# A transformer block on one core: the inverse row sums are scaled as two rows of three read and three rows of two written

## The chip, the cores and the metric

The kernel runs on 1 core of one Trainium2 chip. The metric is the device time of an execution in microseconds (us). One execution was also recorded by the profiler; instruction durations come from that one. In what follows PE is TensorE (PEld is its weight load), DVE is VectorE, ACT is ScalarE, POOL is GpSimd and SP is SyncE, which issues all the DMAs.

## The reference, cut to what matters

For x of 16 batches x 512 tokens x 256 channels:

```
xn = layernorm(x)
q, k, v = xn @ wq, xn @ wk, xn @ wv        # 8 heads of 128
q, k = rope(q), rope(k)
s = q k^T / 128, causal mask               # 512 x 512 per batch and head
p = softmax(s)
attn = (p v) @ wo
ffn = s2 * relu2(s1 * relu2(s0 * [xn, -xn] @ K0) @ K1) @ K2     # K are +1/-1, relu2 is 2 * relu
out = x + attn + ffn
```

The softmax is what the change touches: each row of p is exp(s - max) divided by the sum of the row.

## The kernel before, in words

The core works through 128 groups g = 8b + h, one for each batch b and head h. Precision beyond 16 bits comes from splitting a value into a high and a low fp16 part: ACT writes the high part, DVE the rest, and PE multiplies high by high, high by low and low by high.

Of a group, PE computes q and k (`qk`, whose matmuls are recorded at L277), ACT, DVE and POOL rotate them (L485, L486, L637, L417, L641, L489, L420), and PE forms the scores (`scores`, L763) in four tiles of 128 queries, whose widths are 128, 256, 384 and 512 because of the causal mask. The four tiles i = 0 to 3 of a group lie in three PSUM banks. Then, for the softmax:

- `row_max` (DVE, L665) masks a tile and keeps the row maximum in column i of the four of `MX`, in slot g % 4.
- `row_bias` (ACT, L502) turns the four maxima into the four biases in `NM`.
- `exponent` (ACT, L506) takes the exponential of a tile in place and accumulates the row sums into column i of `SM`.
- `inverse` (DVE, L672 to L676) is a reciprocal of the four sums (L673) and, after a wait for it, a multiplication by 4096 (L675). `RI`, the reciprocals, is the same memory as `NM`, and `RK`, the scaled ones, is that of `MX`. The scaling reads and writes its four values in the order 0, 2, 1, 3, as two rows of two with a stride of two inside a row.
- `p_hi` (ACT, L510) writes the high part of the normalised tile, with the scaled value of the row as its scale; it waits for `inverse` by the semaphore s_inv. `p_lo` (DVE, L679) writes the low part, after the `p_hi` of the same tile.
- SP turns the tiles round by DMA transposes (L325), and PE multiplies by v (`values`, L780). ACT and DVE split the result (`o_hi` L499, `o_lo` L660), and PE projects it with wo (`project`).

Beside this PE works on the feed-forward net: `layer0` (L277), the seven half-size products that stand for the eight of layer 1 (`product`, L812) and `layer2` (L823). The product with wv is also made of seven (`v_product`, L801), and DVE copies or adds its partial sums from bank to bank in between (`copy_v`, L647; `add_v5`, L644). POOL normalises the next batch (L385) and makes its sums (L398 to L403).

Nothing is scheduled at run time. Each engine has one program, written out by hand as a sequence of helper calls with semaphore waits between them; batches 4 to 14 are one loop body. Each engine issues strictly in that order, so what stands behind a slow instruction on its engine waits with it. Two places of the vector program matter below. In the loop body (L4672 and after) the order is

```
copy_v(dve, ps[0], ps[7])
dve.wait_ge(s_exp, 32 * b + 4)
inverse(dve, 8 * b)
dve.wait_ge(s_P_hi, 32 * b + 1)
p_lo(dve, 8 * b, 3, ps[3])
dve.wait_ge(s_vs, 14 * b - 5)
dve.wait_ge(s_ffn, 2 * b)
copy_v(dve, ps[0], ps[6])
```

and a `v_product` of PE waits for that second `copy_v`. In batch 1 to 2, `inverse` of group 12 is followed by a `row_max` and an `o_lo`, and `scores` on PE wait for that `o_lo` to free a bank.

Of the kernel before, what the change touches and what calls it, by code (L numbers as in the profile page):

```python
# [10 lines left out]
ALU = mybir.AluOpType  # L11
ACT = mybir.ActivationFunctionType
# [7 lines left out]
HI, LO = 0, 1  # L20
# [17 lines left out]
def block_kernel(nc, x, wq, wk, wv, wo, k0, k1, k2, s3, cosT, sinT, out):  # L38
    ctx = ExitStack()
    with ctx:  # L40
        def sb(name, shape, dt=F32):
            return ctx.enter_context(nc.sbuf_tensor(name, shape, dt))

        def sem(name):
            return ctx.enter_context(nc.semaphore(name))
# [27 lines left out]
        LESS = HALF[:, 4:5]  # L73
        MX = sb("mx", [128, 4, 4])
        NM = sb("nm", [128, 4, 4])
        SM = sb("sm", [128, 4, 4])
        RI = NM
        RK = MX
        P2 = sb("p2", [128, 4])
        KN = sb("kn", [128, 4])  # L80
        SC = sb("sc", [128, 8])
# [93 lines left out]
        s_exp = sem("s_exp")  # L175
        s_inv = sem("s_inv")
        s_P_hi = sem("s_P_hi")
# [42 lines left out]
        s_recip = sem("s_recip")  # L220
# [22 lines left out]
        def tile_of(ps, i):  # L243
            return ps[:, S_COL[i]:S_COL[i] + WIDTH[i]]

        def part(g, i, s):
            q, row, n = SQUARE[i]
            a = SQ_AT[q] + s * SQ_SIZE[q] + row * n * 128
            return PH[:, g % 2, a:a + WIDTH[i]]
# [251 lines left out]
        def row_bias(act, g):  # L501
            act.activation(NM[:, g % 4, :], MX[:, g % 4, :], ACT.Copy, scale=SC[:, 1:2]).then_inc(s_bias, 1)  # L502

        def exponent(act, g, i, ps):
            p = tile_of(ps, i)
            act.activation(p, p, ACT.Exp, bias=NM[:, g % 4, i:i + 1], scale=SC[:, 0:1],  # L506
                           accum_out=SM[:, g % 4, i:i + 1]).then_inc(s_exp, 1)

        def p_hi(act, g, i, ps):
            act.activation(part(g, i, HI), tile_of(ps, i), ACT.Copy, scale=RK[:, g % 4, i:i + 1]).then_inc(s_P_hi, 1)  # L510

        def keep_r(act, ps):
            act.activation(RT[:, 0:2].rearrange("p a b -> p (a b)"), ps[:, :], ACT.Relu).then_inc(s_r, 1)
# [27 lines left out]
        def stats_end(dve, b):  # L541
            r = b % 2
            for t in range(4):
                mv = dve.bn_aggr(MV[:, r, t, :], BN[:, t, :])
            mv.then_inc(s_mean, 1)
            dve.wait_ge(s_mean, b + 1)
            dve.tensor_scalar(VE[:, r, :], MV[:, r, :, 1], EPS, 2.0 ** -12, ALU.add, ALU.mult).then_inc(s_stats, 1)

        def stats_first(dve):
            for t in range(2):  # L550
                stats_tile(dve, 0, t)
            dve.wait_ge(s_x[0], 16)
            stats_tile(dve, 0, 2)
            stats_tile(dve, 0, 3).then_inc(s_rows, 1)
            dve.wait_ge(s_rows, 1)
            stats_end(dve, 0)

        def stats(dve, b):
            for t in range(4):
                rows = stats_tile(dve, b, t)  # L560
            rows.then_inc(s_rows, 1)
            dve.wait_ge(s_rows, b + 1)
            stats_end(dve, b)
# [102 lines left out]
                                     scalar=-3.0e38, op0=ALU.add, op1=ALU.max,  # L666
                                     accum_out=MX[:, g % 4, i:i + 1]).then_inc(s_max, 1)

        def every_other(v):
            return v.rearrange("p (a b) -> p b a", a=2)  # L670

        def inverse(dve, g):  # L672
            dve.reciprocal(RI[:, g % 4, :], SM[:, g % 4, :]).then_inc(s_recip, 1)  # L673
            dve.wait_ge(s_recip, g + 1)
            dve.tensor_scalar(every_other(RK[:, g % 4, :]), every_other(RI[:, g % 4, :]), 4096.0, None,  # L675
                              ALU.mult).then_inc(s_inv, 1)  # L676

        def p_lo(dve, g, i, ps):
            dve.scalar_tensor_tensor(part(g, i, LO), tile_of(ps, i), RK[:, g % 4, i:i + 1], part(g, i, HI),  # L679
                                     ALU.mult, ALU.subtract).then_inc(s_P_lo, 1)  # L680

        def difference(dve, n, ps):
# [914 lines left out]
        def scalar_program(act):  # L1597
# [107 lines left out]
            v_first_hi(act, 0, 2, BANK[3])  # L1705
            act.wait_ge(s_bias, 1)
            exponent(act, 0, 3, BANK[4])
            exponent(act, 0, 2, BANK[2])
            exponent(act, 0, 0, BANK[2])
            exponent(act, 0, 1, BANK[5])  # L1710
            act.wait_ge(s_v, 2)
            v_first_hi(act, 0, 0, BANK[6])
            act.wait_ge(s_inv, 1)
            p_hi(act, 0, 3, BANK[4])
            p_hi(act, 0, 2, BANK[2])
            act.wait_ge(s_rot, 6)
            qk_hi(act, 2, 1)
            p_hi(act, 0, 0, BANK[2])
            p_hi(act, 0, 1, BANK[5])
            act.wait_ge(s_max, 8)  # L1720
# [1549 lines left out]
            o_hi(act, 127, BANK[5])  # L3270

        def vector_program(dve):
            dve.wait_ge(s_x_first, 16)
            dve.wait_ge(s_x[0], 16)
            stats_first(dve)
# [122 lines left out]
            row_max(dve, 1, 2, BANK[7])  # L3398
            dve.wait_ge(s_exp, 4)
            inverse(dve, 0)  # L3400
            dve.wait_ge(s_crossed, 6)
            dve.wait_ge(s_straight, 6)
            rotate(dve, 2, 1, BANK[1])
            row_max(dve, 1, 0, BANK[7])
            dve.wait_ge(s_P_hi, 1)
            p_lo(dve, 0, 3, BANK[4])
            dve.wait_ge(s_S, 6)
            row_max(dve, 1, 1, BANK[1])
            v_first_lo(dve, 0, 0, BANK[6])
            dve.wait_ge(s_P_hi, 4)  # L3410
            p_lo(dve, 0, 1, BANK[5])
            p_lo(dve, 0, 0, BANK[2])
            p_lo(dve, 0, 2, BANK[2])
            v_first_lo(dve, 0, 2, BANK[3])
            split_w_lo(dve, "v", 4)
            dve.wait_ge(s_exp, 8)
            inverse(dve, 1)
            v_first_lo(dve, 0, 3, BANK[6])
            dve.wait_ge(s_swap, 7)
# [26 lines left out]
            v_first_lo(dve, 1, 2, BANK[4])  # L3446
            dve.wait_ge(s_exp, 12)
            inverse(dve, 2)
            split_w_lo(dve, "v", 5)
            dve.wait_ge(s_o_hi, 1)  # L3450
# [1022 lines left out]
            for b in range(4, 15):  # L4473
                ps = [BANK[i] for i in ROTATION[b]]
# [1999 lines left out]
        @block.vector  # L6474
        def _(e):
            vector_program(e)
# [33 lines left out]
```

## Time and profile before

| | us |
|---|---|
| runs shown (3) | 1725.69, 1727.59, 1727.61 |
| median | 1727.59 |
| the profiled execution's own time | 1725.82 |
| span of its instructions | 1724.0 |
| PE busy in the span | 1701.0 (99%) |
| DVE busy | 1465.5 (85%) |
| ACT busy | 1482.5 (86%) |
| POOL busy | 970.5 (56%) |
| granted TensorE clock, mean | 0.997 of full speed |

A busy PE is not PE at its peak, since matmuls overlap in the pipeline. So a short wait of PE is not to be seen as idle time of PE, but as a larger distance between the starts of two groups of matmuls. The profiled execution lies 1.77 us under the median of the runs shown.

### The profile page before, as it was taken

To read this page: it belongs to the slowest core of one execution; us is meant where nothing else is said; L and a number is where in the kernel's file an instruction comes from. 1 tells how busy PE (TensorE), PEld (TensorE's weight loads), DVE (VectorE), ACT (ScalarE), POOL (GpSimd) and SP (SyncE) were. 2 spreads that over 40 slices of the span, in tenths; PEclk is the share of its full clock that TensorE was granted. 3 is DMA by queue.
4 is the path that set the end of the run, shared out by engine and by line. 5 is a ranking of instruction groups with operands and counts; after the bars stand their busy time and mean duration, and the time that the engine had idled before them with its cause. 6 is when DMAs were issued, how large, how long until landed. Compare 5 with 4: busy or idle time off the path is not lost.

```text
span 1724.0 us, 35729 instructions
## 1 busy us (share of the span) xinstructions
PE 1701.0 (99%) x13340; PEld 1257.8 (73%) x13340; DVE 1465.5 (85%) x3502; ACT 1482.5 (86%) x3250; POOL 970.5 (56%) x775
## 2 busy tenths in 40 slices
PE   7999999999999999999999999999999999999999
PEld 3567767777777687777777777777777777768777
DVE  8998798888988889788897888879888898887975
ACT  6898898888988889888898888888888898888984
POOL 7764647556564565655556465564655656455522
PEclk9999999999999999999999999999999999999999
DMA  5233644534434344453435434344453434434443
GB/s 177 47 71 63 113 77 84 95 62 96 77 83 77 81 80 75 93 75 74 87 73 99 74 80 88 72 82 81 88 83 68 92 74 93 68 80 80 75 83 72
DMA packets 486044, 142.03 MB, mean 82 GB/s; under 512 B 465904, under 2 KB 484848, under 8 KB 485872
## 3 DMA queue, kind: packets, MB, share of 16 engines
q1 hardware_dynamic: 485872, 139.76, 42.5%
q8 instruction: 105, 1.72, 0.4%
q14 instruction: 67, 0.55, 0.1%
HBM read 14.94 MB, written 8.39 MB: 14 GB/s over the span
## 4 chain that ended last, share of the span: by engine, by line
PE 94%; DVE 4%; ACT 1%; DMA 0%; issue 0%; SPq 0%; POOL 0%; DVEq 0%
PE bank L277 35%; PE bank L812 21%; PE bank L780 12%; PE bank L763 11%; PE bank L801 8%; PE bank L823 6%; DVE bank L665 1%; DVE ph L679 0%; ACT bank L506 0%; ACT ph L510 0%; DMA pt<-ph 0%; DVE bank L637 0%; DVE tb L641 0%; PE bank L791 0%; DVE hb L629 0%
## 5 line engine op out<-in xcount | busy, mean ns | idle before, releaser
L417 POOL TENSOR_TENSOR tb<-tb,sin 128x512 f32<-128x512 f32 x256 | 325.7, 1275 | 274.6 <-ACT tb L486 272.8
L420 POOL TENSOR_TENSOR qk<-tb,qk 128x512 f16<-128x512 f32 x256 | 296.7, 1165 | 326.0 <-ACT qk L489 325.8
L812 PE MATMUL bank<-hb,wa 128*128 128x256 f16 x3360 | 382.2, 273 | 0.0
L812 PEld LDWEIGHTS bank<-hb,wa 128*128 128x128 fp8e5 x3360 | 327.5, 98 | 38.9
L506 ACT ACTIVATE bank<-bank,nm,sc 128x512 f32<-128x512 f32 (+3 forms) x512 | 301.3, 589 | 2.9
L679 DVE SCALAR_TENSOR_TENSOR ph<-bank,mx,ph 128x256 f16<-128x256 f32 (+3 forms) x512 | 251.4, 542 | 27.8 <-ACT ph L510 27.1
L510 ACT ACTIVATE ph<-bank,mx 128x512 f16<-128x512 f32 (+3 forms) x512 | 231.0, 537 | 25.8 <-DVE mx L675 25.7
L665 DVE CUSTOM_DVE_ANT_0 bank<-bank,mask 128x128 f32<-128x128 f32 (+3 forms) x512 | 237.1, 513 | 15.4 <-PE bank L763 15.2
L763 PE MATMUL bank<-qk 128*128 128x512 f16 (+3 forms) x1536 | 230.4, 299 | 4.9 <-DVE tb L641 2.6
L780 PE MATMUL bank<-pt,v 128*128 128x256 f16 (+1 forms) x2304 | 229.2, 255 | 1.5 <-DVE hb L692 0.6
L780 PEld LDWEIGHTS bank<-pt,v 128*128 128x128 f16 x2304 | 202.1, 98 | 29.0 <-issue 3.5
L485 ACT ACTIVATE tb<-bank 64x512 f32<-64x512 f32 x256 | 152.2, 594 | 79.8 <-PE bank L277 72.1
L637 DVE TENSOR_TENSOR bank<-bank,cos 128x512 f32<-128x512 f32 x256 | 178.3, 701 | 29.4 <-ACT tb L486 29.0
L763 PEld LDWEIGHTS bank<-qk 128*128 128x128 f16 x1536 | 132.9, 98 | 95.5 <-DVE tb L641 2.8
L489 ACT ACTIVATE qk<-tb 128x512 f16<-128x512 f32 x256 | 160.4, 634 | 33.8 <-PE bank L763 28.5
L277 PE MATMUL bank<-xT,wk 128*128 128x512 f16 x768 | 187.3, 381 | 0.1
L277 PE MATMUL bank<-xT,wq 128*128 128x512 f16 x768 | 186.0, 379 | 0.4 <-DVE ph L679 0.4
L641 DVE TENSOR_TENSOR tb<-bank,tb 128x512 f32<-128x512 f32 x256 | 173.4, 683 | 14.3 <-POOL tb L417 9.9
L277 PE MATMUL bank<-wo,o 128*128 128x256 f16 x1536 | 172.9, 273 | 0.0
L277 PEld LDWEIGHTS bank<-wo,o 128*128 128x128 f16 x1536 | 150.3, 98 | 18.0
L424 POOL TENSOR_TENSOR hb<-rt,hb 128x1024 f16<-128x1024 f32 x60 | 127.9, 2132 | 60.6 <-ACT hb L522 60.6
L486 ACT ACTIVATE tb<-bank 64x512 f32<-64x512 f32 x256 | 150.9, 589 | 3.0
(140 smaller groups left out, 2627.7 us busy)
## 6 DMA issues: line engine op xcount, KB each, us to landing
out<-xnat SPq DMA_DIRECT2D x32, 256.0 KB, 2.1
xnat<-in_x SPq DMA_DIRECT2D x15, 512.0 KB, 3.8
pt<-ph SPq DMA_TRANSPOSE x256, 4.3
o<-in_k SPq DMA_DIRECT2D x1, 1024.0 KB, 7.6
v<-in_wq SPq DMA_DIRECT2D x1, 1024.0 KB, 9.6
v<-in_wk SPq DMA_DIRECT2D x1, 1024.0 KB, 11.5
ph<-in_wv SPq DMA_DIRECT2D x1, 1024.0 KB, 14.0
o<-in_wo SPq DMA_DIRECT2D x1, 1024.0 KB, 10.9
```

The costliest lines, as they stand in the source:

```text
L277: m = pe.matmul(ps[:, cols[0]:cols[1]], l, r, start=start and n == 0, stop=signal is not None and n == last)
L417: pool.tensor_tensor(tb, tb, SIN[:], ALU.mult).then_inc(s_crossed, 1)
L420: pool.tensor_tensor(QK[:, g % 2, 2 * w + 1, :], TB[:, (2 * g + w) % TRING, :], QK[:, g % 2, 2 * w, :], ALU.subtract).then_inc(s_qk_lo, 1)
L506: act.activation(p, p, ACT.Exp, bias=NM[:, g % 4, i:i + 1], scale=SC[:, 0:1], accum_out=SM[:, g % 4, i:i + 1]).then_inc(s_exp, 1)
L510: act.activation(part(g, i, HI), tile_of(ps, i), ACT.Copy, scale=RK[:, g % 4, i:i + 1]).then_inc(s_P_hi, 1)
L637: dve.tensor_tensor(ps[:, :], ps[:, :], COS[:], ALU.mult).then_inc(s_straight, 1)
L641: dve.tensor_tensor(tb, ps[:, :], tb, ALU.add).then_inc(s_rot, 1)
L665: dve.tensor_tensor_reduce(out=s, in0=s, in1=MASK[:, 512 - WIDTH[i]:512], scale=1.0, scalar=-3.0e38, op0=ALU.add, op1=ALU.max, accum_out=M ...
L679: dve.scalar_tensor_tensor(part(g, i, LO), tile_of(ps, i), RK[:, g % 4, i:i + 1], part(g, i, HI), ALU.mult, ALU.subtract).then_inc(s_P_lo, 1)
L763: mm = pe.matmul(ps[:, col:col + w], l, m, start=i == tiles[0] and n == 0, stop=end)
L780: mm = pe.matmul(ps[:, 128 * i0:128 * i1], l, m, start=n == 1, stop=n == 18)
L812: mm = pe.matmul(ps[:, 256 * u:256 * u + 256], WA[:, w, k, (2 * j + u) * 128:(2 * j + u) * 128 + 128], HB[:, h, s, k, :], start=first and ...
```

## The change

`SM`, `RI` and `RK` become buffers of their own. The sums and the reciprocals lie in two rows of four places, of which three are used: tile i is at row i // 3, column i % 3. The reciprocal reads and writes all six used places. The scaling reads them as two rows of three and writes them as three rows of two, so the scaled value of tile i is at row i // 2, column i % 2. Two of the six values belong to no tile; one memset at the start of the vector program makes the whole of `SM` ones. No wait is added, moved or taken away.

```
-        SM = sb("sm", [128, 4, 4])
-        RI = NM
-        RK = MX
+        SM = sb("sm", [128, 4, 2, 4])
+        RI = sb("ri", [128, 4, 2, 4])
+        RK = sb("rk", [128, 4, 3, 4])
...
+        def row_sum(g, i):
+            return SM[:, g % 4, i // 3, i % 3:i % 3 + 1]
+
+        def row_scale(g, i):
+            return RK[:, g % 4, i // 2, i % 2:i % 2 + 1]
...
             act.activation(p, p, ACT.Exp, bias=NM[:, g % 4, i:i + 1], scale=SC[:, 0:1],
-                           accum_out=SM[:, g % 4, i:i + 1]).then_inc(s_exp, 1)
+                           accum_out=row_sum(g, i)).then_inc(s_exp, 1)
...
-            act.activation(part(g, i, HI), tile_of(ps, i), ACT.Copy, scale=RK[:, g % 4, i:i + 1]).then_inc(s_P_hi, 1)
+            act.activation(part(g, i, HI), tile_of(ps, i), ACT.Copy, scale=row_scale(g, i)).then_inc(s_P_hi, 1)
...
+        def unused_sums(dve):
+            dve.memset(SM[:], 1.0)
...
-        def every_other(v):
-            return v.rearrange("p (a b) -> p b a", a=2)
-
         def inverse(dve, g):
-            dve.reciprocal(RI[:, g % 4, :], SM[:, g % 4, :]).then_inc(s_recip, 1)
+            dve.reciprocal(RI[:, g % 4, :, 0:3], SM[:, g % 4, :, 0:3]).then_inc(s_recip, 1)
             dve.wait_ge(s_recip, g + 1)
-            dve.tensor_scalar(every_other(RK[:, g % 4, :]), every_other(RI[:, g % 4, :]), 4096.0, None,
-                              ALU.mult).then_inc(s_inv, 1)
+            dve.tensor_scalar(RK[:, g % 4, :, 0:2], RI[:, g % 4, :, 0:3], 4096.0, None, ALU.mult).then_inc(s_inv, 1)
...
-            dve.scalar_tensor_tensor(part(g, i, LO), tile_of(ps, i), RK[:, g % 4, i:i + 1], part(g, i, HI),
+            dve.scalar_tensor_tensor(part(g, i, LO), tile_of(ps, i), row_scale(g, i), part(g, i, HI),
                                      ALU.mult, ALU.subtract).then_inc(s_P_lo, 1)
...
         def vector_program(dve):
+            unused_sums(dve)
             dve.wait_ge(s_x_first, 16)
```

## Rows read from the trace of the kernel before

**Rows 1.** The page: busy time by engine.
```profile
PE 1701.0 (99%) x13340; PEld 1257.8 (73%) x13340; DVE 1465.5 (85%) x3502; ACT 1482.5 (86%) x3250; POOL 970.5 (56%) x775
```

**Rows 2.** Groups on DVE: busy us, mean ns of one | idle before.
```profile
L675 DVE TENSOR_SCALAR mx<-nm 128x4 f32<-128x4 f32 x128 | 41.4, 323 | 4.4
...
L614 DVE RECIPROCAL kn<-p 128x2 f32<-128x2 f32 x2 | 0.3, 166 | 0.1
...
L568 DVE TENSOR_SCALAR pt<-pt 128x3 f32<-128x3 f32 x1 | 0.2, 199 | 0.0
```

**Rows 3.** Single lines: duration ns min/median/max.
```profile
L675 DVE TENSOR_SCALAR mx<-nm x128: 169/170/1140, 65.5 to 1704.6; 128x4 f32<-128x4 f32 x128
...
L673 DVE RECIPROCAL nm<-sm x128: 160/177/179, 65.3 to 1704.4; 128x4 f32<-128x4 f32 x128
...
L547 DVE TENSOR_SCALAR ve<-mv x16: 170/538/1266, 6.3 to 1554.8; 128x4 f32<-128x4 f32 x16
```

**Rows 4.** Stretches, L675 alone: us, DVE busy (count), clock, DMA share, GB/s.
```profile
864.50:969.50 105.00, 2.85 (x8) 1.00 0.43 79
```

**Rows 5.** Stretches, PE alone: us, PE busy (count), clock, DMA share, GB/s.
```profile
864.50:969.50 105.00, 105.00 (x837) 1.00 0.43 79
```

**Rows 6.** Order of time around 884 us, batch 8: start, duration, engine, line.
```profile
884.15 1.15 POOL L420 TENSOR_TENSOR qk<-tb,qk 128x512 f16<-128x512 f32 x1 [2.11 <-ACT qk L489]
...
884.46 0.87 DVE L675 TENSOR_SCALAR mx<-nm 128x4 f32<-128x4 f32 x1
...
886.09 0.75 DVE L679 SCALAR_TENSOR_TENSOR ph<-bank,mx,ph 128x512 f16<-128x512 f32 x1 [0.76 <-ACT ph L510]
...
886.69 0.82 PE L801 MATMUL bank<-wv,xT 128*128 128x256 f16 x6
886.75 0.69 DVE L647 TENSOR_SCALAR bank<-bank 128x512 f32<-128x512 f32 x1
...
887.50 0.83 PE L801 MATMUL bank<-wv,xs 128*128 128x256 f16 x6
```

**Rows 7.** The chain of waits, batches 0 to 2: start us, us, what.
```profile
84.35 0.61 DVE mx L675
...
95.37 0.93 DVE mx L675
...
119.44 0.65 PE bank L801 x6
...
215.99 1.14 DVE mx L675
```

**Rows 8.** Waits of the weight loads: us in total, times, longest.
```profile
PEld bank L801 <- DVE bank L647: 4.9, 14, 1.3
```

**Rows 9.** Order of time around 84 us.
```profile
84.87 1.29 DVE L617 SCALAR_TENSOR_TENSOR wv<-o,kn,wv 128x512 f16<-128x512 f32 x1
84.89 0.73 POOL L398 TENSOR_TENSOR xs<-xs 128x256 f32<-128x256 f32 x1
...
86.91 1.79 PE L763 MATMUL bank<-qk 128*128 128x512 f16 x12 [0.65 <-DVE o L660]
```

**Rows 10.** Order of time around 96 us and 110 us.
```profile
95.14 0.62 ACT L489 ACTIVATE qk<-tb 128x512 f16<-128x512 f32 x1
...
96.33 1.42 ACT L510 ACTIVATE ph<-bank,mx 128x128 f16<-128x128 f32 x3 [0.56 <-DVE mx L675]
...
110.44 0.81 PE L780 MATMUL bank<-pt,v 128*128 128x256 f16 x6 [0.64 <-DVE hb L692]
```

**Rows 11.** Order of time around 216 us.
```profile
217.18 1.31 ACT L510 ACTIVATE ph<-bank,mx 128x512 f16<-128x512 f32 x3
...
218.39 1.16 PE L763 MATMUL bank<-qk 128*128 128x384 f16 x9 [1.56 <-DVE o L660]
...
218.91 0.47 DVE L679 SCALAR_TENSOR_TENSOR ph<-bank,mx,ph 128x256 f16<-128x256 f32 x1
```

**Rows 12.** The last inverse, order of time.
```profile
1704.61 0.17 DVE L675 TENSOR_SCALAR mx<-nm 128x4 f32<-128x4 f32 x1
```

## The prediction

> **What bounds the kernel now.** I read the page first. PE is busy 99% of the span, DVE and ACT 85% [rows 1], so only a wait that reaches PE costs time. The groups on DVE then show what the change is about: the scaling L675 has 128 instructions of 323 ns on average [rows 2], though the single line gives a median of 170 ns and a maximum of 1140 ns [rows 3]. Most take 170 ns; a few take far longer. The sum over the clean time is 41.4 - 128 x 0.170 = 19.6 us. The reciprocal L673 just ahead of it, as small and also from buffer to buffer, never takes more than 179 ns [rows 3]. The small L547 behaves as the scaling does: 170 at least, 1266 at most [rows 3]. In order of time each long scaling overlaps a POOL instruction: that of 884.46 runs 0.87 us and ends at 885.33, just as the POOL L420 of 884.15 ends (885.30) [rows 6]. So the scaling waits for POOL to finish, the reciprocal doesn't.
>
> The Trainium skill says the same of the engines (VectorE: DVE Perf Modes, "Mode 2×_2P — use both read ports for one tensor"; SBUF — State Buffer, "Who interferes with whom"): a tensor_scalar between SBUF buffers uses a port pair shared with GpSimd, and waits for it, if the outermost dimensions of source and destination are both even, or equal. By that rule the old pattern (two and two) waits, as the rows show, and the new one (two and three) wouldn't.
>
> In the steady part eight scalings take 2.85 us a batch [rows 4], 1.49 over 8 x 0.170: two long ones. Over the same 105.00 us PE is busy 105.00 [rows 5]. There almost all of the DVE time saved is hidden. What is left is read from distances between PE groups, and from the chain for the first three batches, which holds three long scalings [rows 7].
>
> **The steady part.** Around 884.46 the order on DVE is scaling, p_lo (waiting for p_hi on ACT), copy_v. p_lo starts at 886.09 and copy_v right behind it at 886.75, and PE's next v_product starts at 887.50, when copy_v has ended [rows 6]. The v_product before it started at 886.69, a distance of 0.81, where six such matmuls take 0.65 when nothing is waited for [rows 7]: PE lost 0.16 us. With a scaling of about 0.2 us, p_hi, p_lo and copy_v move up by 0.67. p_lo would end near 886.17 and copy_v near 886.8, ahead of the 887.34 at which PE could go on. So this whole 0.16 goes, and the next limit is PE itself. The waits of the weight loads for L647 are 14, 4.9 us in sum, one of 1.3 [rows 8]: the other 13 are alike, 0.28 each (seen at the load, which runs ahead of the matmul), one a batch. 13 x 0.16 = **2.1 us**. The other long scaling of a batch has no distance behind it on PE over the free one: 0.
>
> **The first batches.** Up to 110 us the chain runs mostly on DVE.
> - 84.35: 0.61 us [rows 7], of which 0.44 is waiting. Next on DVE is L617, itself held up: 1.29 us beside POOL's L398 [rows 9]. Started earlier, it would meet the POOL instruction that the scaling met and go behind it, POOL's L398 then waiting instead. It ends some 0.4 to 0.5 earlier, and so do the o_lo behind it and PE's scores at 86.91, which wait for that o_lo [rows 9]. I take 0.45. POOL may lose up to 0.7 us once; its results are next needed by ACT and a transpose, with more than that to spare.
> - 95.37: 0.93 us, 0.76 of it waiting. ACT is busy with L489 to 95.76, so p_hi, now at 96.33, gains 0.57 at most [rows 10]. I take 0.5.
> - PE waits for DVE at 110.44 with 0.64 of visible idle time [rows 10], so both gains arrive there: 0.95. Behind it the stretch to 136 us hangs on PE's own products, which come earlier by as much.
> - 215.99: 1.14 us, 0.97 of it waiting [rows 7]. Behind it on DVE stand a row_max and the o_lo that PE waits for until 218.39, 1.56 of visible idle time [rows 11]. That o_lo moves up by nearly 0.9. But the next steps of PE wait for p_lo of group 12. ACT's p_hi at 217.18 does not move, since ACT has had work all the time before it. PE's `values` wait for the p_lo of 218.91, which ends at 219.38 [rows 11]; without the delayed o_lo in front it would end at about 219.0. Of 0.9, PE keeps **0.4**.
> The other long one there, at 204 us, lies beside a PE that has work.
> Sum of the head: **1.35 us**, between 0.7 (the chain cuts the first two to half, the third to 0.2) and 2.2 (all of 0.44, 0.76 and 0.97).
>
> **What it adds.** The reciprocal has six values for four. Two values take 166 ns and four 173 on average [rows 2, 3], so about 7 ns more. The scaling of six isn't in the trace: at least as now (170), at most the slowest clean small one, 199 ns for three values [rows 2]; I take 185. That is 128 x 22 ns = 2.8 us on DVE, hidden but at some 5 places of the head and the last inverse, whose scaling is clean now (0.17) [rows 12]: 6 x 0.02 = 0.1 us. A gain from a scaling under 170 ns is excluded, as no 4-value one is faster. The memset is one instruction while DVE waits for x: 0. Were x there at once, it would cost what a small instruction does, 0.2. The buffers of their own add no wait and take none away: 0.
>
> **Sum.** 2.1 + 1.35 - 0.1 = 3.35 us of the profiled execution's 1725.82: 1722.5. That execution lies 1.8 us under the median of the runs shown, whose two upper values are 1727.6. I forecast against the median: 1727.59 - 3.35 = **1724.2 us**. A measurement of this kernel can tell about 0.2%, 3.45 us, from no change; the forecast lies on that edge.
>
> **The rivals.**
> - **A, the forecast** (0.60). Scalings free of POOL, 2.6 to 4.1 us gained. Half of it is on either side of 3.45, a little more below it: 0.27 faster, 0.33 same.
> - **B, the head gives all**: 2.1 + 2.2 - 0.1 = 4.2 us, 1723.4. For it: the chain puts all three long scalings on the critical path [rows 7]. Against it: ACT's gapless work at 95.7 and 217.2 [rows 10, 11]. 0.12, faster.
> - **C, given back later**: PE arrives earlier at a wait that now just passes (a transpose, POOL's rotation), and only the steady 2.1 or the head's 1.35 is left: 1725.5 to 1726.2. For it: hundreds of PE waits are met now with a margin that the rows don't show. 0.16, same.
> - **D, the change does not do what it says**: the new pattern waits for POOL as well. The trace has no instruction with unlike patterns; only that L673 escapes shows that size and place are not what makes one wait. Then 1727.59 + 0.1 = 1727.7. 0.09, same.
> - **E, slower**: six values read as rows of three and written as rows of two run as a slow form. The place is the scaling in front of copy_v, once a batch. It lasts 0.87 there now; PE loses nothing while it is under 0.71, loses the present 0.16 at 0.87, and every nanosecond above counts. To be 3.45 slower over 13 batches takes 1.14 us a scaling; the time would be 1731. The nearest small instructions without POOL take 0.2 [rows 2]. 0.03.
>
> **How the numbers follow.** Faster by over 0.2%: 0.27 + 0.12 = 0.39. Same: 0.33 + 0.16 + 0.09 = 0.58. Slower: 0.03. The range: the largest gain, 4.2, taken from the lower runs (1725.7) gives 1721.5; the smallest gain of C, 1.35, from the upper (1727.6) gives 1726.3, and I reach on to 1727.3 for a part of D.
>
> **What would show it.** In the changed kernel the scaling should have a minimum and a maximum close to each other, 170 to 200 ns, and 24 us or less in sum for 41.4; ACT's 0.5 us waits for it shrink. The reciprocal stays under 190. L547 keeps its long ones, being untouched. In a steady batch the two v_products around 886.7 stand 0.65 apart, the weight loads no longer wait for L647, and a batch's period falls by 0.16. In the head PE's group at 110.44 comes at about 109.5. Wrong would be: long scalings that remain (D); a period unchanged though the scalings are short (the wait passed to another instruction, C); a PE wait for copy_v that stays, because copy_v waits for its own product and not for p_lo.

## The result, and the profile after

| | before | changed |
|---|---|---|
| median of 21 runs each, us | 1728.08 | 1725.25 |
| lowest and highest, us | 1725.69, 1730.61 | 1721.22, 1727.03 |
| profiled execution, us (span) | 1725.82 (1724.0) | 1725.58 (1723.8) |
| granted TensorE clock of it | 0.997 | 0.995 |

The ratio of the runs is 0.998, with a 95% interval of 0.9974 to 0.9986: 3.5 us less, between 2.4 and 4.5. The medians differ by 2.83 us. The interval leaves out 1, so the gain is there; but the ratio lies just on the 0.2% that the forecast had as its edge.

The two profiled executions differ by 0.24 us only, so they must be compared stage by stage. First the scaling itself. The page's busy times, then single lines of the changed kernel (duration ns min/median/max; L681 is the scaling, L679 the reciprocal; the line between them is what ACT's p_hi waited for the scaling, us in total and times), and the scaling in one steady stretch (us, DVE busy, clock, DMA share, GB/s):

```profile
PE 1701.2 (99%) x13340; PEld 1259.8 (73%) x13340; DVE 1450.5 (84%) x3503; ACT 1481.1 (86%) x3250; POOL 969.9 (56%) x775
```

```profile
L681 DVE TENSOR_SCALAR rk<-ri x128: 159/160/161, 68.7 to 1704.2; 128x6 f32<-128x6 f32 x128
...
  ACT ph L516: 10.9, 18
...
L679 DVE RECIPROCAL ri<-sm x128: 173/190/192, 68.5 to 1704.0; 128x6 f32<-128x6 f32 x128
```

```profile
864.50:969.50 105.00, 1.27 (x8) 1.00 0.42 79
```

The maximum of the scaling fell from 1140 ns [rows 3] to 161, its mean from 323 [rows 2] to 160, and the eight of a batch take 1.27 us for 2.85 [rows 4]. The 128 scalings take 20.9 us less in sum and the reciprocals 1.6 more; DVE's busy time on the page, where instructions that overlap count once, falls by 15.0. PE is as busy as before [rows 1]. The new memset runs at 0.80 us for 0.09, long before x arrives at 4.34, and costs nothing.

In the kernel before, 29 scalings start with over 0.3 us of a POOL instruction still to run. 27 of them are the long ones, and each of these ends 22 to 25 ns after that POOL instruction; the two others (at 65.5 and 193.9 us, beside POOL's L385) stay short, and why isn't shown. In the changed kernel 29 scalings start so as well, and none takes over 161 ns. (In both kernels 54 reciprocals start beside a POOL instruction, and all are short.) Around the place in front of copy_v (L656 now), in order of time, with POOL's L420 running from 884.93 to 886.08, as long as before:

```profile
884.93 1.15 POOL L420 TENSOR_TENSOR qk<-tb,qk 128x512 f16<-128x512 f32 x1 [2.12 <-ACT qk L489]
885.03 0.18 DVE L679 RECIPROCAL ri<-sm 128x6 f32<-128x6 f32 x1
885.24 0.16 DVE L681 TENSOR_SCALAR rk<-ri 128x6 f32<-128x6 f32 x1
...
886.83 0.69 DVE L656 TENSOR_SCALAR bank<-bank 128x512 f32<-128x512 f32 x1
...
887.46 0.82 PE L806 MATMUL bank<-wv,xT 128*128 128x256 f16 x6
...
888.12 0.82 PE L806 MATMUL bank<-wv,xs 128*128 128x256 f16 x6
```

The scaling is done in 0.16 us while POOL still runs. copy_v ends at 887.52, PE needs it at 888.12, and the two v_products stand 0.66 apart, not 0.81 [rows 6]. The waits of the weight loads for copy_v were 14 with 4.9 us [rows 8]; two are left, the long one and one of 0.3 (us in total, times, longest):

```profile
PEld bank L806 <- DVE bank L656: 1.6, 2, 1.3
```

Then PE as a whole. Both kernels have the same 13340 matmuls in the same order, so the start of the n-th one can be compared. The table has, for each kernel, by how many us PE is later than in the kernel before (a minus: earlier), at ten matmuls that start in the kernel before at the times in the first line. e1 to e10 are the experiments of the next section. (Only differences between columns of a line say something of the change. What comes in the first 81 us differs from execution to execution, as shown below.)

```
at            42    81    87    98   110   218   361  1519  1705  1720
changed     3.17  3.12  2.44  2.05  1.77  1.61  1.61 -0.41 -0.40 -0.28
e1          1.70  3.05  3.06  3.06  3.06  3.06  3.06  3.03  3.04  3.13
e2          1.99  3.35  3.34  3.34  3.34  3.33  3.33  3.25  3.25  3.12
e3          1.98  2.49  2.48  2.48  2.48  2.46  2.46  2.36  2.36  2.21
e4          2.24  2.05  1.36  0.98  0.69  0.51  0.52 -1.46 -1.47 -1.54
e5          2.65  2.61  2.61  2.61  2.61  2.61  2.61  0.59  0.59  0.43
e6          2.39  3.73  3.05  2.66  2.40  2.23  2.23  2.27  2.27  2.14
e7          1.63  0.60 -0.09 -0.47 -0.74 -0.90 -0.90 -2.37 -2.37 -2.47
e8          2.58  2.50  1.81  1.42  1.14  0.97  0.97  3.99  3.98  3.85
e9          1.85 -0.24 -0.93 -1.31 -1.59 -1.76 -1.76 -3.79 -3.80 -3.84
e10         0.88  0.84  0.15 -0.24 -0.52 -0.69 -0.69 -2.47 -2.48 -2.25
```

In the changed kernel PE is 3.12 us late at 81 us and gains from there on: 1.51 by 218 us (0.68, 0.39, 0.28 and 0.16 at the four matmuls of 87, 98, 110 and 218 us), nothing to 361, then 2.02 in twelve steps of 0.167, one a batch and each at the v_product behind copy_v. From 81 us to the end it gains 3.40 us.

**Where the 3.1 us of the first 81 us come from.** Stretches of PE, the kernel before and then the changed one (us, PE busy, granted clock, DMA share, GB/s):

```profile
0.00:45.00 45.00, 33.89 (x152) 0.92 0.50 170
```

```profile
0.00:45.00 45.00, 33.13 (x138) 0.85 0.50 170
```

The granted clock of the first 45 us was 0.92 of full speed in the one and 0.85 in the other: more of that time at 1.2 GHz, for 2.4. In this part PE waits again and again for loads and for DVE, and each trace has stretches at half clock after such waits, in other places and of other length each time. The clock is not all of it. By 14 us PE is 0.9 us late already, at full clock in both: ACT's L439 starts at 11.27 us after 1.04 us of waiting for the load of `in_k`, for 10.37 in the kernel before, where it waited for no load, and the first xT that PE needs comes 0.9 later with it. In the other ten executions of the table the same instruction starts between 10.20 and 11.12. None of this touches an inverse, the first of which comes at 65 us. So the first column of the table, from 0.88 to 3.17, says nothing of the change: the changed kernel itself stands at both ends of it (3.17, and e10 with 0.88).

The 21 runs spread alike: those of the changed kernel with a mean clock of 0.993 took 1726.5 us (mean of 3), with 0.995 1724.0 (4), with 0.997 1722.1 (2). Only the profiled executions show where the low clock lies: within the first 81 us nearly all of it.

### The profile page after: what moved, and what is told of

Its sections match the earlier page's. It is cut to its first block, busy times and chain, and to the rows that moved or that the text cites. A ratio compares the mean times of both kernels' runs of the same rounds, so it can differ in the third digit from the quotient of the medians.

```text
span 1723.8 us, 35730 instructions
## 1 busy us (share of the span) xinstructions
PE 1701.2 (99%) x13340; PEld 1259.8 (73%) x13340; DVE 1450.5 (84%) x3503; ACT 1481.1 (86%) x3250; POOL 969.9 (56%) x775
## 4 chain that ended last, share of the span: by engine, by line
PE 95%; DVE 2%; ACT 1%; DMA 1%; issue 0%; SPq 0%; DVEq 0%
PE bank L277 36%; PE bank L817 21%; PE bank L785 12%; PE bank L768 12%; PE bank L806 8%; PE bank L828 6%; DMA o<-in_k 0%; PE bank L796 0%; DVE bank L674 0%; ACT bank L512 0%; ACT ph L516 0%; DMA pt<-ph 0%; DVE ph L684 0%; DVE hb L638 0%; DVE rt L689 0%
## 5 line engine op out<-in xcount | busy, mean ns | idle before, releaser
L420 POOL TENSOR_TENSOR qk<-tb,qk 128x512 f16<-128x512 f32 x256 | 296.9, 1166 | 326.2 <-ACT qk L489 326.0
L684 DVE SCALAR_TENSOR_TENSOR ph<-bank,rk,ph 128x256 f16<-128x256 f32 (+3 forms) x512 | 251.5, 543 | 27.8 <-ACT ph L516 27.1
L516 ACT ACTIVATE ph<-bank,rk 128x512 f16<-128x512 f32 (+3 forms) x512 | 231.0, 538 | 11.1 <-DVE rk L681 10.9
L489 ACT ACTIVATE qk<-tb 128x512 f16<-128x512 f32 x256 | 160.2, 633 | 33.8 <-PE bank L768 28.5
```

Of the source, the lines that this page charges most:

```text
L420: pool.tensor_tensor(QK[:, g % 2, 2 * w + 1, :], TB[:, (2 * g + w) % TRING, :], QK[:, g % 2, 2 * w, :], ALU.subtract).then_inc(s_qk_lo, 1)
L684: dve.scalar_tensor_tensor(part(g, i, LO), tile_of(ps, i), row_scale(g, i), part(g, i, HI), ALU.mult, ALU.subtract).then_inc(s_P_lo, 1)
```

## The experiments

All start from the changed kernel unless said otherwise. Most were timed by one execution, whose time says little when those of one kernel differ by up to 5 us; for these the trace and the table carry the reading.

**e1: buffers of their own, nothing else** (edited from the kernel before)

```
         SM = sb("sm", [128, 4, 4])
-        RI = NM
-        RK = MX
+        RI = sb("ri", [128, 4, 4])
+        RK = sb("rk", [128, 4, 4])
```

> The kernel before, with buffers of their own for the reciprocals and the scaled values, and nothing else; the scaling keeps its two rows of two. My theory (the pattern does it): the scaling keeps its long ones, 16 to 18 of over 0.5 us, about 41 us in sum as before, the v_product behind copy_v stays 0.81 us behind the one before it, and the time is that of before. Rival (sharing memory with NM and MX made the scaling wait): all 128 at 0.16 to 0.17 us, 21 us in sum.

One execution of 1728.93 us, the kernel before beside it at 1728.07 (median). Single line, as above:

```profile
L675 DVE TENSOR_SCALAR rk<-ri x128: 169/170/1136, 67.2 to 1707.6; 128x4 f32<-128x4 f32 x128
```

28 scalings over 0.3 us (27 in the kernel before; the 16 to 18 over 0.5 of my expectation were a miscount, it is 27 in both), 42.1 us in sum, and the line e1 of the table stays at 3.03 to 3.13 from 81 us to the end. Sharing memory had nothing to do with it, and the buffers alone move nothing.

**e2: patterns alike, two rows of three; e3: alike, three rows of two**

```
-        RK = sb("rk", [128, 4, 3, 4])
+        RK = sb("rk", [128, 4, 2, 4])
...
-            return RK[:, g % 4, i // 2, i % 2:i % 2 + 1]
+            return RK[:, g % 4, i // 3, i % 3:i % 3 + 1]
...
-            dve.tensor_scalar(RK[:, g % 4, :, 0:2], RI[:, g % 4, :, 0:3], 4096.0, None, ALU.mult).then_inc(s_inv, 1)
+            dve.tensor_scalar(RK[:, g % 4, :, 0:3], RI[:, g % 4, :, 0:3], 4096.0, None, ALU.mult).then_inc(s_inv, 1)
```

e3 keeps `RK` and makes `SM` and `RI` three rows as well, of which two places each are used:

```
-            dve.reciprocal(RI[:, g % 4, :, 0:3], SM[:, g % 4, :, 0:3]).then_inc(s_recip, 1)
+            dve.reciprocal(RI[:, g % 4, :, 0:2], SM[:, g % 4, :, 0:2]).then_inc(s_recip, 1)
...
-            dve.tensor_scalar(RK[:, g % 4, :, 0:2], RI[:, g % 4, :, 0:3], 4096.0, None, ALU.mult).then_inc(s_inv, 1)
+            dve.tensor_scalar(RK[:, g % 4, :, 0:2], RI[:, g % 4, :, 0:2], 4096.0, None, ALU.mult).then_inc(s_inv, 1)
```

> The changed kernel, but the scaling writes two rows of three, as it reads them: six values, own buffers, ones in the unused sums, and the patterns alike with an even outermost count. My theory (only unlike outermost counts keep the scaling clear of POOL): long scalings come back, 0.9 us at most of those in a steady batch, 1.5 us over the clean time a batch; the clean ones take 0.17, not 0.16; the time is that of the kernel before, 3 us over the changed one. Rival (six values, or rows that don't touch, are enough): all at 0.16, time of the changed kernel.

> The changed kernel with three rows of two on both sides of the scaling: the outermost counts are odd and equal. By the Trainium skill's rule (both even, or equal) it waits for POOL again: long ones of 0.9 us in a steady batch, 41 us in sum or little over. Rival (an odd outermost count on either side is enough to stay clear): all at 0.16, 20.4 us in sum.

e2 took 1727.99 us (median of 10), a ratio to the kernel before of 0.9999 (0.999 to 1.0009). e3, one execution, took 1728.02. Their scalings:

```profile
L681 DVE TENSOR_SCALAR rk<-ri x128: 170/171/1124, 67.5 to 1707.9; 128x6 f32<-128x6 f32 x128
...
  ACT ph L516: 35.0, 44
```

```profile
L681 DVE TENSOR_SCALAR rk<-ri x128: 169/170/1124, 67.5 to 1707.0; 128x6 f32<-128x6 f32 x128
```

Six values, own buffers and gaps between the rows are all there, and the whole gain is gone: the table's lines e2 and e3 are flat. Even and alike waits, odd and alike waits too. Both have 40 long scalings, 50.7 and 50.5 us in sum, more than the 41 I had expected of e3; all 80 end 24 to 31 ns after a POOL instruction. A third one a batch waits (766 ns at 941.36 in e2), which in the kernel before is clean (169 ns at 938.05). There POOL is between two instructions just as the scaling arrives, and the scaling arrives 0.02 us later behind the start of its reciprocal (0.23 for 0.21), which takes longer with six values; POOL's next one starts 0.24 behind it in both. That those 0.02 us decide which goes first is a guess and was not tried.

**e4: the patterns turned round**, three rows of two read (`SM` and `RI` have three rows, as in e3) and two rows of three written (`RK` has two, as in e2):

```
-            dve.tensor_scalar(RK[:, g % 4, :, 0:2], RI[:, g % 4, :, 0:3], 4096.0, None, ALU.mult).then_inc(s_inv, 1)
+            dve.tensor_scalar(RK[:, g % 4, :, 0:3], RI[:, g % 4, :, 0:2], 4096.0, None, ALU.mult).then_inc(s_inv, 1)
```

> The changed kernel with the patterns turned round: the scaling reads three rows of two and writes two rows of three. My theory (only the inequality of the outermost counts matters): all 128 at 0.16 us, 20.4 us in sum, time and chain as of the changed kernel. Rival (an even count on the reading side is what keeps clear, or the writing side alone decides): long ones as before, 40 of over 0.3 us.

```profile
L681 DVE TENSOR_SCALAR rk<-ri x128: 158/159/161, 67.8 to 1703.2; 128x6 f32<-128x6 f32 x128
```

1724.28 us in one execution, and from 81 us to the end PE gains 3.59 us, as in the changed kernel. So it is the inequality that counts, not the side. Together with e2 and e3 this agrees with the Trainium skill's condition (VectorE: DVE Perf Modes, "Mode 2×_2P — use both read ports for one tensor"). Counts that are both even but unequal were not tried. And with six values the rows differ in length whenever they differ in number, so these runs can't tell a rule on the number of rows from one on any unlike shape.

**e5: the new pattern in one scaling a batch (that of group 8b, from batch 3 on); e6: in all the others**

```
+        def free(g):
+            return g % 8 == 0 and g >= 24
...
+            to = RK[:, g % 4, :, 0:2] if free(g) else RL[:, g % 4, :, 0:3]
+            dve.tensor_scalar(to, RI[:, g % 4, :, 0:3], 4096.0, None, ALU.mult).then_inc(s_inv, 1)
```

`row_scale` reads `RK` or `RL` by the same condition; e6 has `not (...)`.

> The changed kernel, in which only the scaling of group 8b in front of copy_v, from batch 3 on, has the new pattern; all others read and write two rows of three. My theory: that one scaling a batch carries the whole steady gain. The distance of the two v_products falls from 0.81 to 0.65, 0.16 a batch, 12 times 0.167 = 2.0 us; the other long one of a batch (0.95 us) stays and costs nothing; the gains of the first 110 us are missing (1.4 us), so the time lies between the two kernels, 1.4 us over the changed one. Rival (both long scalings of a batch matter): less than 0.16 gained a batch.

> The complement of the run with one a batch: the scaling in front of copy_v from batch 3 on reads and writes two rows of three, all the others have the new pattern. My theory: the gains of the first 220 us are there (1.6 us), the steady gain is missing, so 12 distances of 0.81 between the v_products remain and this run ends 2.0 us later than the changed kernel on equal clocks. Rival (the other long one of a batch also carried a part): less than 0.16 lost a batch.

One execution each, 1726.23 and 1727.94 us. The table tells more: e5 stands at 2.61 up to 361 us and is at 0.59 at 1519, a gain of 2.02, all in the steady part, from 13 scalings with the new pattern and 115 with that of e2. e6 gains 1.50 from 81 to 218 us (3.73 to 2.23) and then stands still to 1705. 2.02 and 1.50 make 3.52, for the 3.40 and 3.59 of the two full ones. In e6 the scaling in front of copy_v and the v_products of batch 8 are as before:

```profile
886.72 0.86 DVE L688 TENSOR_SCALAR rl<-ri 128x6 f32<-128x6 f32 x1
...
888.94 0.82 PE L813 MATMUL bank<-wv,xT 128*128 128x256 f16 x6
...
889.75 0.83 PE L813 MATMUL bank<-wv,xs 128*128 128x256 f16 x6
```

0.81 again, and so (0.81 or 0.82) in all 12 batches from 3 to 14, for 0.65 or 0.66 in the changed kernel and e5. Of the 128 scalings, 12 carry the steady gain, one a batch.

**e7 and e8: a delay in front of that scaling**, 13 times in all: in batches 3 to 14 and, beyond the 12 that I had counted, in the last:

```
+            if g % 8 == 0 and g >= 24:
+                dve.memset(IDLE[:, 0:400], 1.0)
             dve.tensor_scalar(RK[:, g % 4, :, 0:2], RI[:, g % 4, :, 0:3], 4096.0, None, ALU.mult).then_inc(s_inv, 1)
```

`IDLE` is 480 fp16 values wide; e8 fills all of it, once before the reciprocal and once here.

> The changed kernel with one memset of 400 fp16 values on DVE between reciprocal and scaling of group 8b, from batch 3 on (12 in all): some 0.45 us of delay. PE would reach the v_product behind copy_v 0.54 us after copy_v is ready (888.12 less 0.06 less 887.52). My theory: the slack takes it all, the v_products stay 0.65 apart, nothing is lost. Rival (the whole DVE delay comes through, since DVE is 84% busy): 12 times 0.45 = 5.4 us more.

> The same with two memsets of 480 fp16 values, one ahead of the reciprocal and one ahead of the scaling: some 1.0 to 1.1 us of delay. My theory: 0.54 of it is taken by the slack, so PE loses 0.5 to 0.55 us a batch, 12 times that = 6 to 7 us; each waiting nanosecond over the slack counts. Rival (none comes through, PE has other work): the time of the changed kernel. Other rival (all comes through): 12 to 13 us.

The memsets took 392 ns, and twice 458; in batch 8 the scaling ends 0.37 us late in e7 and 0.95 in e8, measured from the start of the reciprocal or, for e8, of the copy_v ahead of both memsets. e7 keeps its v_products 0.65 or 0.66 apart in all 12 batches:

```profile
884.95 0.82 PE L809 MATMUL bank<-wv,xT 128*128 128x256 f16 x6
...
885.61 0.60 PE L809 MATMUL bank<-wv,xs 128*128 128x256 f16 x4
```

Its steady gain is 1.47 us for 2.02, but none of the 0.55 is lost at this place: 0.38 is one single wait of `values` for a transpose at 1062 us, which no other execution here has (e10 loses 0.18 to one like it at 538 us). e8:

```profile
888.92 0.82 PE L811 MATMUL bank<-wv,xT 128*128 128x256 f16 x6
...
889.99 0.83 PE L811 MATMUL bank<-wv,xs 128*128 128x256 f16 x6 [0.25 <-DVE bank L657]
```

1.07 apart, 0.42 lost; by the table e8 loses 3.02 us between 361 and 1519 us where the changed kernel gains 2.02, a difference of 5.04, which is 12 times 0.42. A delay of 0.95 less a loss of 0.42 is a slack of 0.53, for 0.54 by the rows of the changed kernel. I had expected 0.5 to 0.55 lost, the memsets having been estimated too long. So a delay of 0.37, under the slack, costs nothing, and of one of 0.95 all that is over the slack is lost.

**e9: the same for the variances.** The other small scaling that waits for POOL (L547 of [rows 3]) gets the same pattern; POOL's power behind it still takes four values. The two unused places of `MV` are made ones, and what reads `MV` and `VE` finds its values at the new places.

```
-        MV = sb("mv", [128, 2, 4, 2])
-        VE = sb("ve", [128, 2, 4])
+        MV = sb("mv", [128, 2, 2, 4, 2])
+        VE = sb("ve", [128, 2, 3, 4])
...
-            dve.tensor_scalar(VE[:, r, :], MV[:, r, :, 1], EPS, 2.0 ** -12, ALU.add, ALU.mult).then_inc(s_stats, 1)
+            dve.tensor_scalar(VE[:, r, :, 0:2], MV[:, r, :, 0:3, 1], EPS, 2.0 ** -12, ALU.add, ALU.mult).then_inc(s_stats, 1)
```

> The changed kernel, and the same pattern for the other small DVE instruction that waits for POOL, the variance scaling of the next batch (L553 there: 0.17 at least, 1.27 at most): it reads two rows of three and writes three rows of two. My theory: all 16 take 0.16, so the one of 1.27 us at 65.6 us ends 1.1 us earlier; it stands on the chain in front of the rotation that PE waits for (2.64 us of visible idle time). PE is 0.9 to 1.1 us earlier from there on, nothing more is gained in the steady part, where the variance is not waited for: some 1.0 us under the changed kernel, 4.4 under the one before. Rival (given back in the first 110 us at the next wait, on ACT's exponentials or POOL's rotation): less than 0.3 us.

> The changed kernel itself, timed on the same chip beside the one before and the run with the variance scaling. 3.4 us (0.2%) under the kernel before by the median, with each kernel's own runs spread over some 4 us as the TensorE clock of the first 75 us falls out; at equal granted clock the difference is 3 to 4 us.

| | median, us | ratio to before, interval |
|---|---|---|
| before (16 runs) | 1728.36 | |
| changed (11 runs) | 1725.10 | 0.998, 0.9971 to 0.9988 |
| e9 (6 runs) | 1722.76 | 0.9968, 0.9956 to 0.998 |

e9 is 2.3 us under the changed kernel by the medians; the intervals overlap a little. Its trace, order of time, behind the single line:

```profile
L554 DVE TENSOR_SCALAR ve<-mv x16: 160/161/161, 6.2 to 1551.0; 128x6 f32<-128x6 f32 x16
```

```profile
64.26 0.16 DVE L554 TENSOR_SCALAR ve<-mv 128x6 f32<-128x6 f32 x1
66.41 0.69 DVE L653 TENSOR_TENSOR tb<-bank,tb 128x512 f32<-128x512 f32 x1
67.15 0.22 PEld L771 LDWEIGHTS bank<-qk 128*128 128x128 f16 x3 [1.77 <-DVE tb L653]
67.16 0.50 PE L771 MATMUL bank<-qk 128*128 128x256 f16 x3 [1.60 <-DVE tb L653]
```

PE's idle time in front of those scores is 1.60 us. In the changed kernel it is 2.64:

```profile
69.52 0.82 PE L768 MATMUL bank<-qk 128*128 128x256 f16 x3 [2.64 <-DVE tb L650]
```

So 1.04 us were gained there, as expected. The rest is the clock. PE's stretches from 60 to 81 us, the changed kernel timed again (e10) and e9:

```profile
60.00:81.00 21.00, 17.93 (x109) 0.92 0.24 46
```

```profile
60.00:81.00 21.00, 18.62 (x123) 1.00 0.30 57
```

After the wait of 2.64 us PE ran for a while at half its clock (1.2 GHz): the matmuls of k behind it start 427 ns apart, where they take 216 otherwise. After the one of 1.60 us it did not, and that is worth 1.0 us more; e9 goes from 1.85 in the table at 42 us to -0.24 at 81. It isn't shown that the shorter wait is the reason: in e7 the wait was as long as ever (2.65), and the clock stayed at 1.00 too. From 81 us on e9 gains 3.60 us, no less than the changed kernel, so the rival (given back in the first 110 us) falls. Of the 2.3 us by the medians, then, 1.04 are shown to be the pattern's.

## Why the prediction was right

By its own steps:

- **What the scaling waits for, and that the new pattern ends it** (0.88 given to A, B and C together): right. e1 to e4 take the change apart: not the buffers, not the six values, not the gaps, only the unlike patterns do it.
- **The steady part, 2.1 us**: 2.02, by 12 places of 0.167 and not 13 of 0.16. The thirteenth wait of 0.28 stayed, so it wasn't the scaling's. The reading of it, that 0.16 of 0.70 us reaches PE and a slack hides the rest, is shown by e5, e6, e7 and e8: the point from which the scaling costs PE, 0.71 us long by rival E, is 0.16 + 0.53 = 0.69.
- **The head, 1.35 us**: 1.51, but not as summed. At 87 us 0.68 for 0.45, at 98 and 110 us together 0.67 for 0.5. L617 (L626 now) behaved as drawn: beside the POOL instruction that the scaling had waited for it takes 1.03 us, and POOL's L398 takes 1.18 for 0.73 [rows 9]:

```profile
87.49 0.16 DVE L681 TENSOR_SCALAR rk<-ri 128x6 f32<-128x6 f32 x1
87.57 1.03 DVE L626 SCALAR_TENSOR_TENSOR wv<-o,kn,wv 128x512 f16<-128x512 f32 x1
...
88.01 1.18 POOL L398 TENSOR_TENSOR xs<-xs 128x256 f32<-128x256 f32 x1
```

The scaling gives back the 0.44 of the prediction, and L617, which lasted 1.29, another 0.26 that the prediction had not counted. At the second place ACT set the bound, as said, but the bound of 0.57 was misread: p_hi starts 0.10 before the end of L489, in the changed kernel 0.52 after a start of L489 that lasts 0.62. So p_hi moved up by 0.67, and all of it reached PE.
- **The third place of the head, 0.4 us, is the step that failed**: 0.16. I had the row_max behind the scaling start at once. In the changed kernel DVE stands idle for 0.70 us in front of it. The kernel before, then the changed one:

```profile
216.02 0.81 PE L763 MATMUL bank<-qk 128*128 128x512 f16 x3
...
217.04 0.69 DVE L665 CUSTOM_DVE_ANT_0 bank<-bank,mask 128x512 f32<-128x512 f32 x1
```

```profile
217.79 0.81 PE L768 MATMUL bank<-qk 128*128 128x512 f16 x3
...
218.64 0.70 DVE L674 CUSTOM_DVE_ANT_0 bank<-bank,mask 128x512 f32<-128x512 f32 x1 [0.70 <-PE bank L768]
...
220.00 1.16 PE L768 MATMUL bank<-qk 128*128 128x384 f16 x9 [1.40 <-DVE o L669]
```

It needs scores that PE has only just made: it starts 0.04 us after they end (218.60), where it started 0.21 after them (216.83) in the kernel before. The difference, 0.17, is what PE gains. The long scaling had covered a wait for PE; the question "what is late next" was put to ACT and not to the instruction right behind.

- **What it adds**: a scaling of six takes 160 ns. I had excluded anything under 170. The alike six of e2 take 170 or more, so the ten nanoseconds belong to the pattern, not to the count. The reciprocal takes 186 for 173, twice what I took. No loss of PE is seen from either, so the term of 0.1 us was one too many.
- **Rival B** (all of the head, 2.2 us) and **C** (given back): 1.51 arrived, and no later wait took it back. **D** is ruled out by the 161 ns, **E** by the same.
- **The sum**: 3.35 us forecast, 3.40 in the trace from 81 us on, 3.09 in the repeated one (e10), 3.5 by the ratio and 2.83 by the medians. That it came within 0.05 of the trace is in part luck: two places of the head were put 0.40 us too low together and 0.1 was taken off that nothing cost; against that the third place was put 0.24 too high and the steady part 0.08, and 0.12 was lost in the last 20 us, which scatter by more than that from execution to execution (the last two columns of the table). The time, 1724.2 for 1725.25, is 1.05 off: 0.49 since the median of the kernel before is 1728.08 over 21 runs and not the 1727.59 of three, and 0.52 since the medians differ by less than 3.35. The ratio lies on the 0.2% that divided "faster" from "same", so this result can't tell how good 0.39 against 0.58 was.

## What to carry to other kernels

A very short instruction whose mean is far above its median may wait for something that no semaphore shows; put the long ones beside what the other engines do in that moment. The small scaling here, from SBUF to SBUF on DVE, takes turns with POOL when source and destination are both two rows or both three, and doesn't when one is two rows of three and the other three rows of two; the two dummy values that this takes cost nothing that reached PE. But count what of it reaches the engine that is the bound: here 21 us of scalings were worth 3.4, at four places of the first 220 us and one a batch behind them, and the places were to be found from distances between PE's groups, not from idle times.

## What the runs showed that I had not expected

- The free form is also the shorter one: 160 ns for 170, clean against clean, with six values each (changed and e2).
- Alike patterns of six values wait for POOL 40 times, those of four values 27 or 28 times; the places are the same, but for one more a batch.
- The profiled executions differ most in the first 81 us, by PE's clock and by when a load arrives. The eleven whose first 81 us hold nearly the same work (the kernel before and all of the table but e9) reach that point at times that differ by up to 3.7 us, as much as the whole change brings; a change of this size is seen in one pair of traces only after that part is set aside.
